# First products of a group spread over its slots in an attention and expert block

## What is computed

```
h   = gelu(einsum('bhwd,edf->bhwef', gn(x), W1) + b1)      # 8 experts, 96 -> 384
x1  = x + einsum('bhwef,efo->bhweo', h, W2) ... * gates    # 384 -> 96, top 2 of 8
t   = x1 + attention(layernorm(x1))                        # 6 heads, causal
out = t + experts(layernorm(t))                            # the same with 4 experts, top 2 of 4
```

## Time and profile before

| what | value |
|---|---|
| median of three runs | 1364.79 us (1362.82 to 1364.9) |
| the profiled execution | 1360.14 us, span 1358.2 us |
| PE busy | 1233.0 us, 91% |
| ACT busy | 996.6 us, 73% |
| DVE busy | 807.8 us, 59% |
| POOL busy | 801.5 us, 59% |
| TensorE clock granted, mean over the span | 0.976 of full speed |

### The profile page before, as it was taken

The page is one execution under the profiler, slowest core; times in us unless marked ns, Lnnn a source line. Parts: engine busy times, 40 slices in busy tenths (PEclk is TensorE's granted clock), DMA queues, the critical chain, the costliest instruction groups (busy, mean ns, idle before and its releaser), DMA issues.

```text
span 1358.2 us, 32919 instructions
## 1 busy us (share of the span) xinstructions
PE 1233.0 (91%) x12573; PEld 718.2 (53%) x12573; DVE 807.8 (59%) x2517; ACT 996.6 (73%) x2024; POOL 801.5 (59%) x815
## 2 busy tenths in 40 slices
PE   5988879999999999999999999999999988988987
PEld 2655552566536664466635665366644652462455
DVE  4784683478716784377735776178843782582343
ACT  4968548787887878877786878867787767746775
POOL 5967552667727784477816776276834662442566
PEclk9998898999999999999999999999999998997989
DMA  6002100300021000400012000310003000300100
GB/s 123 13 1 51 22 2 25 73 1 2 13 61 38 2 2 26 84 2 2 2 51 57 2 2 14 72 26 2 2 25 72 1 2 13 73 1 14 26 8 18
DMA packets 38159, 34.77 MB, mean 26 GB/s; under 512 B 26859, under 2 KB 28780, under 8 KB 38002
## 3 DMA queue, kind: packets, MB, share of 16 engines
q1 hardware_dynamic: 21362, 26.37, 9.2%
q10 hardware_dynamic: 16640, 6.29, 1.8%
HBM read 22.62 MB, written 9.63 MB: 24 GB/s over the span
## 4 chain that ended last, share of the span: by engine, by line
PE 59%; DVE 15%; ACT 9%; issue 6%; POOL 4%; DMA 2%; SPq 2%; DVEq 2%; POOLq 1%; ACTq 1%
PE ps_y L683 22%; PE ps_u L683 19%; PE ps_r L683 10%; PE ps_m L683 7%; POOL hidl L661 4%; DVE mpart L1215 3%; ACT hidh L975 3%; DVE acc L1164 3%; ACT xn L989 2%; DVE yt L1348 2%; ACT hid L974 2%; PE ps_m L702 1%; POOLq L641 1%; SPq L545 1%; ACT probs L1014 1%
## 5 line engine op out<-in xcount | busy, mean ns | idle before, releaser
L661 POOL TENSOR_TENSOR hidl<-hid,hidh 128x512 f16<-128x512 f32 x576 | 682.2, 1200 | 246.0 <-ACT hidh L975 238.4
L974 ACT ACTIVATE hid<-ps_u 128x512 f32<-128x512 f32 x576 | 344.9, 599 | 256.0 <-PE ps_u L683 246.4
L683 PEld LDWEIGHTS ps_y<-w2s,hidh 128*128 128x128 f16 x4608 | 276.7, 98 | 143.9 <-issue 7.9
L975 ACT ACTIVATE hidh<-ps_u 128x512 f16<-128x512 f32 x576 | 343.1, 596 | 0.0
L1215 DVE TENSOR_REDUCE mpart<-ps_r 128x1 f32<-128x512 f32 (+2 forms) x576 | 296.8, 549 | 73.4 <-PE ps_r L683 64.8
L683 PE MATMUL ps_y<-w2s,hidh 128*128 128x96 f16 x4608 | 323.7, 207 | 0.8 <-DVE acc L1164 0.8
L683 PE MATMUL ps_y<-w2s,hidl 128*128 128x96 f16 x2304 | 226.2, 208 | 3.2 <-POOL hidl L661 2.4
L623 POOL TENSOR_SCALAR_AFFINE_SELECT probs<-probs 128x384 f32<-128x384 f32 x128 | 66.6, 521 | 258.6 <-ACT probs L1014 258.4
L683 PE MATMUL ps_r<-ks,qs 96*128 96x512 f16 (+2 forms) x576 | 181.9, 329 | 19.3 <-DVE mpart L1215 13.2
L683 PE MATMUL ps_y<-probs,vaug 128*32 128x512 f32 (+3 forms) x1152 | 165.3, 510 | 1.4 <-issue 0.8
L1014 ACT ACTIVATE probs<-ps_r 128x512 f32<-128x512 f32 (+3 forms) x352 | 153.1, 511 | 18.0 <-PE ps_r L683 17.7
(11 more groups left out here) (187 smaller groups left out, 1420.3 us busy)
## 6 DMA issues: line engine op xcount, KB each, us to landing
rb<-rsum_dram SPq DMA_DIRECT2D x24, 256.0 KB, 4.3
qs<-qk_dram SPq DMA_DIRECT2D x48, 96.0 KB, 3.1
ks<-qk_dram SPq DMA_DIRECT2D x48, 96.0 KB, 3.9
xin<-in_x_dram ACTq DMA_DIRECT2D x8, 384.0 KB, 3.6
qk_dram<-qk_h SPq DMA_DIRECT2D x16, 192.0 KB, 2.1
qk_dram<-qk_l SPq DMA_DIRECT2D x16, 192.0 KB, 2.3
out_dram<-xo ACTq DMA_DIRECT2D x8, 384.0 KB, 2.9
w_raw<-in_L_conv_W_dram SPq DMA_DIRECT2D x8, 288.0 KB, 5.0
```

What stands on the lines that cost most here:

```text
L661: g.tensor_tensor(hidl[:, grp.k % HB, j, :], hid[:, j, :], hidh[:, grp.k % HB, j, :], ALU.subtract).then_inc(hl_ready, 1)
L683: return nc.tensor.matmul(dst, lhsT, rhs, start=start, stop=stop, skip_group_check=True)
L974: a.activation(hid[:, j, :], bank[:], ACT.Gelu, scale=1.0 / WS)
L975: a.activation(hidh[:, grp.k % HB, j, :], bank[:], ACT.Gelu, scale=1.0 / WS).then_inc(h_ready, 1)
```

## The change

In the PE block of `moes` the first-product tiles of a group move inside their slots. Tile 0 stays where it is. Tile 1 is issued behind the second-product tile of its slot. Tile 2 is issued behind the second-product tile and behind the chores of its slot.

```diff
--- before.py
+++ after.py
@@ -777,10 +777,12 @@
                         pe.wait_ge(zeroed_late, 1)
                     for slot in slots:
                         j = slot % TC
-                        if up and j < HT:
+                        if up and j == 0:
                             first_layer(it, up, j)
                         if older and j < 2:
                             second_layer(older, grp.k - 2, 2 + j)
+                        if up and j == 1:
+                            first_layer(it, up, j)
                         if down and j >= 2:
                             if j == 2 and early and not up:
                                 soft_scores(Image(it, -1), 0)
@@ -792,6 +794,8 @@
                             for i in (j - 2,) if up or j == 2 else (1, 2, 3):
                                 second_layer(down, grp.k - 1, i)
                         run_chores(m, chore, chores(it, phase, slot))
+                        if up and j == 2:
+                            first_layer(it, up, j)
                     older = down if up else None
                     if up:
                         grp.k += 1
```

## The result

| | before | changed |
|---|---|---|
| median, us | 1362.66 | 1371.07 |
| lowest and highest of 17 runs each | 1360.36 to 1369.94 | 1367.9 to 1383.53 |
| the profiled execution: span, us | 1358.2 | 1371.7 |

The changed kernel is slower by a factor of 1.0065 (95% interval 1.005 to 1.0081), 8.4 us by the medians (8.9 by the factor). Forecast were +6.25 us and 1371.0.

A forecast was written before the change was run, and what follows sets the result against it. PE was taken as the bound, issuing back to back outside some 5% of waiting. Five full iterations at +0.95 (4.75) + 0.5 + 0.7 + 0.3 = +6.25 us, on 1364.8 giving 1371.0; 8 in 10 range 1363 to 1377.

The forecast's parts named there:

- (a): Eighth group of a full iteration: tile 0 of the second product waits for POOL, ninth group starts later; +0.3 us.
- (b): Ninth to thirteenth group: later ACT copies and table loads delay DVE and PE's wait at the gates; +0.55 us with (a).
- (c): Fourth and fifth dense group: POOL's subtractions beside DVE's xal hold up tile 0 of the second product; +0.2 us.
- (d): Seventh dense group: tile 2 no longer covers PE's wait for DVE's maxima, which come 0.34 earlier; +0.3 us.
- (e): Start of a full iteration, second group: moved work would fill tile 2's wait for ACT, but DVE limits it; −0.1 us.
- absorbed: Rival: delays of (a) to (d) end in waits for something else, above all DVE; about +1, 1366 us; chance 0.21.
- Second iteration: Iteration where DVE or chains of small steps were said to set the pace; taken as 0, between −1 and +1 us.
- First iteration: PE's wait for the gates until 29.16 us loses tile 2 as cover; +0.7 us taken, between 0 and 1.3.
- Last three: Eighth, ninth and tenth iteration with the end: 0.5 + 0 + 0 + 0.3 = 0.8 us.
- The 0.5 of the eighth iteration: Eighth iteration: said to have the same chores as a full one less the group norm; 0.5 us taken.
- theory A: Formed after the result: PE's third-slot chore precedes tile 2, ACT's ps_m copy still follows its Gelus; ps_m's next user waits.

The follow-up runs named there:

- e5: The whole change only in the five full iterations (it = 2 to 6), the old order elsewhere; 1362.39 us, ratio 1.0000 to the kernel before.
- e3_tile2_alone: The kernel before with only tile 2 moved, behind the second-product tile and chores of its slot; tile 1 stays in front; 1370.68 us, ratio 1.0066.
- e7: The whole change in the second iteration alone (it = 1), the old order elsewhere; 1366.64 us, ratio 1.0033 to the kernel before.
- e8: The kernel before with tile 2 moved in only four groups of the second iteration (slots 10, 14, 18, 22); 1365.62 us, ratio 1.002.
- e12: The change in the second iteration alone, with ACT's third-slot copies out of ps_m there ahead of the Gelus of tile 2; 1363.73 us, ratio 1.0006.
- e4: The changed kernel with ACT's third-slot copies out of ps_m run ahead of the Gelus of tile 2; 1368.1 us, ratio 1.0042 to the kernel before.
- e11: The changed kernel, but tile 2 stays ahead of its slot's chores wherever one uses ps_m; 1364.29 us, ratio 1.0005 to the kernel before.
- e6_not_full: The whole change in all but the five full iterations (it = 0, 1, 7, 8, 9), the old order in those; 1371.05 us, ratio 1.005.
- e10_last_three: The whole change in the last three iterations alone (it = 7, 8, 9), the old order elsewhere; 1364.67 us, ratio 1.0013.

## Why the prediction was right, and where it was not

The number was right, 1371.0 for 1371.07, and the sign. That it was so close is luck, twice over. The base of 1364.79 us, the median of three runs, lay 2.1 us above the median of all 17 (1362.66), and the forecast change was 2.2 us below the measured one (6.25 against 8.4); the two errors cancel. And the change was made up of the wrong terms: of the forecast 6.25 us, 4.75 lay in iterations where no cost can be measured (e5), and of the measured loss most lies where the forecast had 0 to 0.8.

**Full iteration, (a).** Tile 0 of the second product waits for POOL in the eighth group, and the first subtraction of the ninth group comes 0.28 us later against that of the eighth. Forecast +0.3.

**(b), as far as ACT's chain.** By the eleventh group the delay is 0.94 us; forecast 0.95 for ACT's table chain. DVE's next start behind its wait for PE moves from 458.59 to 465.62, which is 0.56 us against the eighth group; forecast 0.55.

```profile
465.62 0.69 DVE L1219 TENSOR_REDUCE mpart<-ps_r 128x1 f32<-128x512 f32 x1 [0.58 <-PE ps_r L683]
```

The step that failed is the next: "Its start moves by 0.55, and so does this wait's end." The wait's end moved by 473.18 - 467.10 = 6.08 us where the eighth group had moved by 6.47: it ends 0.4 us earlier, not 0.55 later, and the wait is gone. DVE's chain was not rigid. In the kernel before, its product `firstc` takes 1.08 us. DVE, before:

```profile
463.01 1.08 DVE L1130 TENSOR_TENSOR firstc<-firstc,secondc 128x64 f32<-128x64 f32 x1
```

It started inside a subtraction of POOL and ended with it. POOL, before (three subtractions, 1.2 us each):

```profile
462.86 3.62 POOL L661 TENSOR_TENSOR hidl<-hid,hidh 128x512 f16<-128x512 f32 x3 [0.86 <-ACT hidh L975]
```

In the changed kernel it starts just ahead of a subtraction and takes 0.23 us. DVE, and below it POOL:

```profile
470.09 0.23 DVE L1134 TENSOR_TENSOR firstc<-firstc,secondc 128x64 f32<-128x64 f32 x1
```
```profile
470.10 2.44 POOL L661 TENSOR_TENSOR hidl<-hid,hidh 128x512 f16<-128x512 f32 x2 [0.30 <-ACT hidh L979]
```

This is not chance in one iteration: `firstc` takes 1.07 to 1.08 us in each of the five full iterations of the kernel before and of the six other kernels with the old order there, and 0.22 to 0.23 in each of the changed kernel, `e3_tile2_alone` and `e5_full_only`.

**A stall that I did not price.** Before `project` the kernel before waits 0.56 us for `yt`. DVE's two products take 2.08 and 1.57 us there; now they take 1.21 and 1.57, and the wait is gone. The duration view of `yt`, before:

```profile
L1348 DVE TENSOR_TENSOR yt<-yt,rb x2: 1573/1824/2076, 421.5 to 424.2; 96x1024 f32<-96x1024 f32 x2
```

and after:

```profile
L1352 DVE TENSOR_TENSOR yt<-yt,rb x2: 1209/1392/1574, 428.7 to 430.5; 96x1024 f32<-96x1024 f32 x2
```

The first of the two started at 421.55, when POOL was busy until 418.89 + 3.66 = 422.55 us; the new one starts at 428.73, when POOL's subtraction has 0.13 us to go (427.70 + 1.16 = 428.86). Both end 1.08 us behind the end of that subtraction, at 423.63 and 429.94. POOL, before and after:

```profile
418.89 3.66 POOL L661 TENSOR_TENSOR hidl<-hid,hidh 128x512 f16<-128x512 f32 x3 [0.65 <-ACT hidh L975]
```
```profile
427.70 1.16 POOL L661 TENSOR_TENSOR hidl<-hid,hidh 128x512 f16<-128x512 f32 x1 [0.48 <-ACT hidh L979]
```

From the fourth to the sixth group the iteration loses 0.71 and gains 1.35 us: -0.64 net. What makes the +0.71 I did not follow.

**(c) and (d).** From the third to the fifth dense group +0.18, forecast +0.2; POOL holds up PE there. From the seventh to the eighth +0.30, forecast +0.3: PE waits for the maxima, and tile 2 is behind that wait. PE at both places:

```profile
507.12 0.30 PE L683 MATMUL ps_y<-w2s,hidl 128*128 128x96 f16 x3 [1.24 <-POOL hidl L661]
...
522.00 0.33 PE L840 MATMUL ps_m<-ident,mtop 128*128 128x128 f32 x1 [0.61 <-DVE mtop L1225]
```

**(e).** -0.21 from the first to the third group, forecast -0.1.

So (a), (c), (d) and (e) hold to about 0.1 us, and (b) failed at its end; all are offset by two gains of DVE that nothing in the working allowed for. The rival *absorbed* comes nearer to the full iterations in size than the forecast does, but not by its reason: the delay reached DVE's chain and was made good inside it, by shorter instructions. That these two collisions make the difference is read from the traces; no run takes them away alone.

**Second iteration.** The step that failed: "For the second, ninth and tenth iteration, where DVE or chains of small steps set the pace, I take 0, between −1 and +1 each." It costs 4.5 us (e7). Of it, the four tiles of e8 make 2.7, and with ACT in PE's order 0.0006 of the 0.0033 is left (e12). PE's waits for the bank lengthen that iteration, from 145.4 to 149.2 us with four tiles moved. The working followed ACT's copy, in (b), only as the source of DVE's data, never as what empties `ps_m`.

**First iteration.** Forecast +0.7, 0 to 1.3; measured 3.9 (1.0 to 6.8), and +4.3 in the traces, where the slowest of the old order (84.0 us) lies below the fastest of the new (86.5). The mechanism was right (tile 2 no longer covers the wait before the bias chore) and shows as 0.2 to 1.8 us by the third group; the term was too small in that it left out the clock behind the wait, some 1.4 us in seven of nine kernels, and the wait for DVE's `xcl`.

**Last three.** Forecast +0.8, measured +1.8 (-0.4 to 4.1), which does not tell it from nothing. The 0.5 of the eighth iteration was taken from the full ones, but it has no dense groups. One part is the same as in the second iteration: in the tenth, the second turn waits 1.12 us for the first to be emptied, where the kernel before does not wait.

```profile
1323.87 0.40 PE L702 MATMUL ps_m<-ident,xn 128*96 128x128 f32 x2 [1.12 <-DVE xal L1111]
```

How the rest is shared out stays open.

**Why e4 brought back only 3 us.** It changes nothing in the first iteration, and in the full ones its trace is 3 us longer than that of the changed kernel (789.0 against 785.9). There it moves ACT's copies in slots 2 and 42, and `firstc` takes 1.02 to 1.03 us again in each of the five, 0.8 more than in the changed kernel. That would make up the 3 us, but it is not tested, and e11, with 1.08, has the shortest full iterations of all.

## What to carry to other kernels

When instructions of one engine are reordered, list for every shared buffer that the moved ones pass not only who fills it but who empties it, and where that stands in the order of the emptying engine: an order that two engines share is part of the kernel. Breaking it on one side cost 2.7 us (0.7 to 4.8) in four tiles out of 192, where the whole change in the five long iterations cost nothing that could be measured. A total that comes out right proves none of its terms; the change switched on by iteration showed in five kernels that the largest one, 4.75 us, was not there. An elementwise instruction may change its own length when the order around it shifts, so a chain of them is not rigid. And work that stands ahead of a wait may have a second worth: without it the tensor clock stayed low behind the wait in all five kernels here, with it in two of nine.

## What the runs showed of the hardware

**A DVE instruction can wait out a POOL instruction.** `firstc`, 64 columns, takes 0.23 us, and 1.08 if it starts 0.15 us into a subtraction of POOL: it ends at 464.09, that subtraction at about 462.86 + 1.2 = 464.06. The Trainium skill ("SBUF — State Buffer", Who interferes with whom) has it that the later of the two is blocked until the earlier ends; the rows agree. The prediction used this for POOL's delay and not for DVE's. DVE's two collisions, 0.85 and 0.87 us, are the largest differences among the rows read here.

**ACT keeps its order.** ACT's copy had its input by 118.05 us and ran at 119.70, behind two Gelus whose product came later. The Trainium skill ("PSUM — Partial Sum Buffer", Engine vs sequencer instructions) calls ScalarE's queue strictly first in, first out; that is all that theory A needs.

**The clock differs between executions of one order.** In the eighth iteration the changed kernel has a granted clock of 0.50 (the last number but two of the line) from 1105.5 to 1111 us, behind a wait of 2.65 us.

```profile
1105.50:1111.00 5.50, 5.39 (x31) 3.13 (x32) 3.19 (x10) 1.38 (x3) 1.15 (x1) 0.50 0.01 3
```

The kernel before has 1.00 behind a wait of 2.58 us at the same place, 1098 to 1105 us:

```profile
1098.00:1105.00 7.00, 6.34 (x70) 4.22 (x71) 6.32 (x20) 4.19 (x8) 3.47 (x3) 1.00 0.01 2
```

With the old order there, `e5_full_only` has 0.81 in 1096 to 1105 us, behind a wait of 2.58 us as well, and its eighth iteration takes 135.0 us where the other old ones take 133.1 to 133.4. So some 1.6 us of the difference between two traces can be the clock. All three kernels with the new order in the eighth iteration have such a low stretch (0.50 above, 0.81 over 9 us in `e6_not_full` and `e10_last_three`), and so part of their +2.8 us may be the clock.
